# Four buffers instead of two for gathered rows, and an uneven split of the gathers between GpSimd and TensorE, in a four-layer graph network

## The chip, the core and the metric

The kernel runs on one core of a Trainium2 chip. The metric is device time in microseconds (us), the median of several executions. PE is TensorE, DVE VectorE, ACT ScalarE, POOL GpSimd and SP SyncE. The time before is 4519.79 us, the median of 3 runs (4518.19 to 4523.56).

## The reference, cut to what matters

There are 3125 nodes with 16 features and 100000 edges sorted by destination. Four layers follow each other, each on a layer-normed input and added to x:

```python
x = x + L0(h)   # edge network: message = h[src] times a 16x16 matrix made from the edge's attributes
x = x + L1(h)   # message = silu(tensor product of h[dst] and 8 edge attributes); summed by src
# L2: two relational convolutions
x_src = x[src]
msg   = sum over r of where(edge_type == r, x_src @ W[r], 0)
norm  = 1 / max(cnt[dst, edge_type], 1)
agg   = segment_sum(msg * norm, dst)
out   = agg + x @ root + bias
# L3
x   = features * out_deg ** -0.5
agg = zeros.at[dst].add(x[src]) * in_deg ** -0.5
```

So each phase gathers a row per edge by one index, weighs it, and sums it by another index.

## The kernel before, in words

The edges form 800 tiles of 125 edges, and 8 tiles form a chunk, so that there are 100 chunks and 50 pairs of chunks. The five phases are l0, l1, l2a, l2b (the two relational convolutions) and l3. Each walks over the 100 chunks. An even chunk uses slot s = 0 of the double-buffered tiles and an odd chunk uses slot s = 1.

The row of an edge reaches SBUF in one of two ways. A "far" tile is gathered by POOL with one indirect DMA of 125 rows (`gathers`, L610 to L626). A "near" tile is gathered on TensorE (`near_rows`, L785): a one-hot of the node's block of 25 nodes (made by DVE in `near_begin`, L1348, as bf16, L1354) times the node table split in three bf16 parts gives 25 candidate rows in PSUM, with 6 matmuls for a tile. DVE halves the candidates four times with predicated copies (`near_finish`, L1360, L1375) by the bits of the node's number. In l2a and l2b the near rows are then spread by edge type (L1409), turned by PE (`near_turn`, L800), copied by ACT (`near_copy`, L1023) and multiplied with the relation's weights by PE (`near_messages`, L807). For the far tiles of l2a and l2b the table in DRAM holds rows that are already multiplied. In l3 ACT copies the near rows into the tile of gathered rows (`near_place`, L1038). How many of a chunk's 8 tiles are near, for even and odd chunks, stands in `NEAR_OF` (L24); `far` (L291) is 8 less that.

For each chunk DVE weighs the rows into `msg` (L1585 near, L1588 far), splits them in three bf16 parts (`split`, L1264; its steps are called msg, hi, rest, mid, low) and spreads them into `stationary` (`to_stationary`, L1285, three instructions). Then PE adds the chunk to `acc` with 24 matmuls (`add_chunk`, L638). PE's order for chunk c in l2a and l2b is: additions of tiles 0 to 3, `near_turn(c+2)`, additions of tiles 4 and 5, `near_rows(c+3)`, additions of tiles 6 and 7, `near_messages(c+2)` (L839 to L852). DVE's order is: the chunk's own work, `is_lo` of c+1 (L1238), `near_finish(c+2)` with `near_begin(c+3)` between its steps (L1424).

Three waits set when POOL gathers for chunk c. The row numbers of c must have arrived (L615); SP loads them after all gathers of c-2 have landed (L431), in its own order after the fields of c-1, which wait for the step low of c-3 (L504), and the keys of c+1 (L499 to L509). And DVE must have read the slot's rows of c-2 (L618): that is the step msg in l2a and l2b, and the step low in l3 (`ROWS_READ`, L331). The loops over chunks have two unrolled chunks ahead, a body of two chunks, and the last four chunks unrolled (`near_chunks`, L359), for POOL none unrolled at the end (`all_chunks`, L341).

## Time and profile before

| | us |
|---|---|
| median of 3 runs | 4519.79 |
| the profiled execution | 4505.11 |
| its span, from the first to the last instruction | 4503.3 |
| PE busy | 4352.7 (97%) |
| DVE busy | 4112.4 (91%) |
| ACT busy | 3226.9 (72%) |
| POOL busy | 3272.0 (73%) |

The page lists the busy time of each engine, the busy share in 40 equal slices of the span, the chain of work that ended last, and the costliest groups of instructions with the idle time before them and what ended it. Five phases follow each other: l0 to about 1388 us, l1 to about 2279 us, l2a from 2337 to 3073 us, l2b from 3092 to 3825 us and l3 from 3841 to 4498 us. Only the last three are touched by the change.

### The profile page before, as it was taken

Reading aid. Unit: us, or ns where it says so; the run is one execution under the profiler, and the core shown is the slowest. Engines: PE = TensorE matmul, PEld = TensorE weight load, DVE = VectorE, ACT = ScalarE, POOL = GpSimd, SP = SyncE. Lnnn points to the kernel's source line nnn. Section 1 sums busy time; section 2 is a strip of 40 time slices with the busy share of each in tenths; the row PEclk is TensorE's granted clock in tenths of the full one; section 3 lists DMA queues with packets and bytes.
Section 4 is the critical chain, followed back from the end, with each engine's and each line's share of the span. In section 5 each row is a group of like instructions: output and inputs, shape, how many; then the busy total and the mean of one; then the engine's idle time right before and its main releaser. Section 6 shows DMA issues by size and latency. Waiting matters only on the chain.

```text
span 4503.3 us, 107817 instructions
## 1 busy us (share of the span) xinstructions
PE 4352.7 (97%) x30477; PEld 3243.1 (72%) x30477; DVE 4112.4 (91%) x11864; ACT 3226.9 (72%) x5359; POOL 3272.0 (73%) x2516
## 2 busy tenths in 40 slices
PE   6999999999997999999989999999999999799999
PEld 4777777777775777777757777776777777566666
DVE  7999999999997999999969999997999998788988
ACT  5777777777774777777737777776777777677777
POOL 6788888888884777777727776765777676688887
PEclk8999999999998999999989999999999999899999
DMA  2111111111112222222211111111111111111111
GB/s 59 28 17 18 18 17 18 17 18 17 18 17 50 62 61 61 61 61 61 61 36 27 27 27 26 28 27 40 28 27 28 27 27 22 32 30 31 31 30 26
DMA packets 337473, 148.67 MB, mean 33 GB/s; under 512 B 250582, under 2 KB 323074, under 8 KB 337434
## 3 DMA queue, kind: packets, MB, share of 16 engines
q0 software_dynamic: 104000, 59.31, 10.3%
q1 hardware_dynamic: 233434, 88.89, 8.0%
q8 instruction: 19, 0.31, 0.0%
q14 instruction: 20, 0.16, 0.0%
HBM read 135.45 MB, written 9.80 MB: 32 GB/s over the span
## 4 chain that ended last, share of the span: by engine, by line
PE 88%; DVE 5%; issue 3%; ACT 2%; DMA 1%; POOL 1%; SPq 0%; POOLq 0%; DVEq 0%; ACTq 0%
PE acc L638 42%; PE rows_ps L795 19%; PE rows_ps L725 7%; PE bank L811 5%; PE bank L725 4%; PE rows_ps L645 3%; PE eaT_ps L803 3%; DVE raw L1309 2%; PE rows_ps L713 2%; PE eaT_ps L701 1%; PE rows_ps L642 1%; ACT stack L970 1%; DVE ea_rest L1192 1%; ACT distances L911 0%; PE bank L671 0%
## 5 line engine op out<-in xcount | busy, mean ns | idle before, releaser
L638 PE MATMUL acc<-one_hot,stationary 125*128 125x392 bf16 x12000 | 2336.9, 329 | 38.5 <-issue 23.8
L622 POOL DMA_INDIRECT gathered<-table_l,row_numbers x1200 | 1601.8, 1335 | 433.6 <-issue 348.0
L638 PEld LDWEIGHTS acc<-one_hot,stationary 125*128 125x128 bf16 x12000 | 1156.0, 100 | 714.1 <-issue 45.7
L911 ACT ACTIVATE distances<-count_hi,fields 125x392 bf16<-125x392 f16 (+1 forms) x2500 | 1223.3, 558 | 0.0
L1285 DVE TENSOR_TENSOR stationary<-mask,parts 125x1024 bf16<-125x1024 bf16 x1500 | 944.1, 684 | 0.0
L896 ACT CAST mask<-is_lo 125x1024 bf16<-125x1024 f32 x500 | 522.2, 1044 | 528.1 <-issue 348.5
L622 POOL DMA_INDIRECT fields_all<-table_l,row_numbers x500 | 640.7, 1281 | 258.8 <-issue 123.2
L1257 DVE TENSOR_SCALAR one_hot<-count_hi,fields 125x392 bf16<-125x392 f16 x2300 | 740.8, 344 | 13.6 <-issue 13.5
L1375 DVE COPY_PREDICATED rows_ps<-near_bits_now,rows_ps 125x320 f32<-125x320 int8 (+3 forms) x1600 | 580.9, 363 | 161.9 <-PE rows_ps L795 119.7
L622 POOL DMA_INDIRECT gathered<-table_l2a,row_numbers x400 | 511.8, 1280 | 283.0 <-DVE parts L1267 117.5
L795 PE MATMUL rows_ps<-node_parts,h1T 125*125 125x192 bf16 (+1 forms) x7200 | 672.5, 251 | 21.5 <-DVE node_parts L1339 19.8
L795 PEld LDWEIGHTS rows_ps<-node_parts,h1T 125*125 125x125 bf16 x7200 | 655.4, 137 | 51.2 <-DVE node_parts L1339 20.0
L622 POOL DMA_INDIRECT gathered<-table_l2b,row_numbers x400 | 511.7, 1279 | 240.8 <-DVE parts L1267 115.3
L924 ACT ACTIVATE one_hot<-distances,ones 125x1568 bf16<-125x1568 bf16 (+1 forms) x400 | 674.0, 1685 | 6.6
L1028 ACT COPY h1T<-eaT_ps 128x500 f32<-128x500 f32 (+1 forms) x300 | 162.5, 542 | 345.3 <-PE eaT_ps L803 335.2
L1309 DVE TENSOR_REDUCE raw<-product 125x32 f32<-125x512 f32 x400 | 395.5, 1009 | 0.0
L725 PE MATMUL rows_ps<-w,h1T 128*125 128x256 f32 x1600 | 386.1, 385 | 7.6 <-DVE product L1302 5.8
L725 PE MATMUL bank<-w,h1T 128*125 128x256 f32 x1600 | 379.5, 380 | 0.0
L725 PEld LDWEIGHTS rows_ps<-w,h1T 128*125 128x125 f32 x1600 | 294.4, 189 | 57.4 <-DVE product L1302 7.4
L725 PEld LDWEIGHTS bank<-w,h1T 128*125 128x125 f32 x1600 | 301.8, 189 | 45.9
L1354 DVE TENSOR_SCALAR h1T<-near_key,node_key 125x500 bf16<-125x500 f16 (+1 forms) x800 | 317.8, 398 | 2.6 <-DMA near_key<-near_keys_by_chunk 2.5
L983 ACT ACTIVATE h1T<-rows_ps,b 128x500 f32<-128x500 f32 x400 | 249.3, 674 | 89.2 <-PE rows_ps L713 86.0
(216 smaller groups left out, 4704.6 us busy)
## 6 DMA issues: line engine op xcount, KB each, us to landing
near_key<-near_keys_by_chunk SPq DMA_DIRECT2D x300, 122.1 KB
gathered<-table_l,row_numbers POOLq DMA_INDIRECT x1200
fields<-edge_fields SPq DMA_DIRECT2D x500, 31.2 KB
near_key<-near_keys_by_chunk SPq DMA_DIRECT2D x100, 91.6 KB
fields_all<-table_l,row_numbers POOLq DMA_INDIRECT x500
gathered<-table_l2a,row_numbers POOLq DMA_INDIRECT x400
gathered<-table_l2b,row_numbers POOLq DMA_INDIRECT x400
ea<-in_edge_attr SPq DMA_DIRECT2D x100, 62.5 KB
```

The source lines that it names most:

```text
L622: pool.indirect_dma_start(out=gathered[ph][:, s, t, :], in_=table[ph], out_offset=None, in_offset=bass.IndirectOffsetOnAxis(ap=row_numbers ...
L638: mm = pe.matmul(acc[:, :], stationary[:, s, k, t, :, :].rearrange("p a b -> p (a b)"), one_hot[:, s, t, :], start=first and t == 0 and k ...
L725: mm = pe.matmul(bank[2 + q % 2][0:EP, j * HID:(j + 1) * HID], h1T[:, half, t * EP:(t + 1) * EP], w2[:, half, :], start=half == 0, stop=ha ...
L795: mm = pe.matmul(near_rows_ps[ph][s][:, t, 0:end - first, :].rearrange("p a f -> p (a f)"), near_one_hot[s][:, g, t * EP:(t + 1) * EP], pa ...
L896: act.copy(mask[:, s].rearrange("p t a f -> p (t a) f"), is_lo[:, s].rearrange("p t a -> p (t a)")[:, :, None].to_broadcast([EP, T * LO, F ...
L911: ins = act.activation(distances[:, i * n:(i + 1) * n], count_hi[:, 0:n], ACT.Abs, scale=-1.0, bias=fields[:, s, k, t:t + 1].bitcast(F32))
L924: act.activation(into, distances[:, 0:into.shape[1]], ACT.Relu, scale=-1.0, bias=ones[0:EP, 0:1]).then_inc(scalar_hot, 1)
L1257: dve.tensor_scalar(one_hot[:, s, t, :], count_hi[:, :], scalar_field(s, hi_field[ph], t), None, ALU.is_equal)
L1285: ins = dve.tensor_tensor(stationary[:, s, k], mask[:, s], source[:, s, :, k * F:(k + 1) * F][:, :, None, :].to_broadcast([EP, T, LO, F]), ...
L1309: dve.tensor_reduce(raw[:, s, 2 * q:2 * q + 2, :], product[:, q % 2].rearrange("p t i o -> p t o i"), AX.X, ALU.add).then_inc(products_sum ...
L1354: ins = dve.tensor_scalar(near_one_hot[s][:, g, 0:n], near_key[:, s, 0:n], node_key[:, g:g + 1], None, ALU.is_equal)
L1375: return dve.copy_predicated(into, chosen, source)
```

## The change

`gathered2`, the tile into which the rows of l2a, l2b and l3 are gathered, gets four slots instead of two, and chunk c uses slot c mod 4. POOL therefore waits for DVE's reading of chunk c-4 and not of c-2. There is one semaphore for each of the four slots, shared by the three phases. All other double-buffered tiles, the row numbers and fields among them, keep two slots. To know its slot of four at build time, every engine's loop over the chunks of these three phases now has a body of four chunks, with four chunks unrolled ahead and four behind (POOL: none behind). The odd chunks of l2a and l2b have three near tiles instead of four, so POOL gathers five tiles for them.

```diff
-NEAR_OF = {"l0": (0, 0), "l1": (3, 3), "l2a": (4, 4), "l2b": (4, 4), "l3": (4, 4)}
+QUADS = CHUNKS // 4
+NEAR_OF = {"l0": (0, 0), "l1": (3, 3), "l2a": (4, 3), "l2b": (4, 3), "l3": (4, 4)}
...
+class Slot(int):
+    def __new__(cls, four, quad):
+        self = int.__new__(cls, four % 2)
+        self.four, self.quad = four, quad
+        return self
+    def two_ago(self):
+        return Slot((self.four + 2) % 4, self.quad if self.four >= 2 else self.quad - 1)
...
-        rows2 = sb("gathered2", [ROWS, 2, T, F])
+        rows2 = sb("gathered2", [ROWS, 4, T, F])
...
+        def rows_in_by(ph, pair, s):
+            if ph not in FOUR_SLOTS:
+                return 16 * far(ph, s) * (pair + 1)
+            earlier = FOUR_SLOTS[:FOUR_SLOTS.index(ph)]
+            return 16 * QUADS * sum(far(k, s) for k in earlier) + 16 * far(ph, s) * (s.quad + 1)
...
+        def fours(eng, body, first, end, tail):
+            for chunk in range(4 * first):
+                body(chunk, chunk // 2, Slot(chunk % 4, chunk // 4))
+            with eng.Fori(first, end) as quad:
+                for j in range(4):
+                    body(4 * quad + j, 2 * quad + j // 2, Slot(j, quad))
+            for chunk in range(CHUNKS - tail, CHUNKS):
+                body(chunk, chunk // 2, Slot(chunk % 4, chunk // 4))
...
-        def near_chunks(eng, body):
+        def near_chunks(eng, body, ph="l1"):
+            if ph in FOUR_SLOTS:
+                fours(eng, body, 1, QUADS - 1, 4)
+                return
...
-                    sp.wait_ge(S[ph]["rows_in"][s], 16 * far(ph, s) * pair)
+                    if ph in FOUR_SLOTS:
+                        sp.wait_ge(S[ph]["rows_in"][s.two_ago().four], rows_in_by(ph, pair, s.two_ago()))
+                    else:
+                        sp.wait_ge(S[ph]["rows_in"][s], 16 * far(ph, s) * pair)
...
-                    if later(chunk, 2):
-                        pool.wait_ge(S[ph]["step"], done(ph, ROWS_READ[ph], chunk - 2))
+                    ahead = 4 if ph in FOUR_SLOTS else 2
+                    if later(chunk, ahead):
+                        pool.wait_ge(S[ph]["step"], done(ph, ROWS_READ[ph], chunk - ahead))
...
-                            out=gathered[ph][:, s, t, :], in_=table[ph], out_offset=None,
+                            out=gathered[ph][:, rows_slot(ph, s), t, :], in_=table[ph], out_offset=None,
...
-                all_chunks(pool, body)
+                if ph in FOUR_SLOTS:
+                    fours(pool, body, 1, QUADS, 0)
+                else:
+                    all_chunks(pool, body)
...
-                    dve.wait_ge(S[ph]["rows_in"][s], 16 * n * (pair + 1))
-                    st.mark(dve.tensor_tensor(msg[:, s, 0:n, :], gathered2[:, s, 0:n, :],
+                    dve.wait_ge(S[ph]["rows_in"][s.four], rows_in_by(ph, pair, s))
+                    st.mark(dve.tensor_tensor(msg[:, s, 0:n, :], gathered2[:, s.four, 0:n, :],
```

The calls of `near_chunks` on SP, PE, ACT and DVE pass the phase. The readers and writers of `gathered2` in l3 (`near_place`, the wait for the rows, `split`) take the slot of four in the same way.

## Rows read from the trace of the kernel before

**Rows 1.** The page, busy time of each engine over the span.
```profile
PE 4352.7 (97%) x30477; PEld 3243.1 (72%) x30477; DVE 4112.4 (91%) x11864; ACT 3226.9 (72%) x5359; POOL 3272.0 (73%) x2516
```

**Rows 2.** Stretches of l2a and l3: length, busy by engine, PE clock, DMA share, GB/s.
```profile
2400.00:3000.00 600.00, 600.00 (x4934) 469.00 (x4933) 556.40 (x1808) 433.54 (x658) 421.09 (x329) 1.00 0.17 27
...
3900.00:4450.00 550.00, 529.30 (x4119) 380.62 (x4118) 495.07 (x1546) 426.34 (x688) 440.85 (x344) 1.00 0.19 31
```

**Rows 3.** Chain of waits inside l2a: start us, us, what (parts of one chunk).
```profile
2408.81 2.00 PE acc L638 x12
2410.81 0.43 PE eaT_ps L803 x4
...
2412.23 2.06 PE rows_ps L795 x24
...
2415.29 0.78 PE bank L811 x8
```

**Rows 4.** POOL in l2a: start, us, operation, idle before and its releaser.
```profile
2705.30 1.48 POOL L622 DMA_INDIRECT gathered<-table_l2a,row_numbers  x1 [0.30 <-issue]
...
2711.11 1.21 POOL L622 DMA_INDIRECT gathered<-table_l2a,row_numbers  x1 [1.29 <-DVE parts L1267]
```

**Rows 5.** POOL in the first chunks of l2a, and DVE's first wait for rows.
```profile
2337.62 1.21 POOL L622 DMA_INDIRECT gathered<-table_l2a,row_numbers  x1 [72.45 <-DMA table_l2a<-stage]
...
2343.77 1.21 POOL L622 DMA_INDIRECT gathered<-table_l2a,row_numbers  x1 [0.30 <-issue]
2344.93 0.23 DVE L1588 TENSOR_TENSOR msg<-gathered,edge_norm 125x64 f32<-125x64 f32 x1 [2.18 <-DMA gathered<-table_l2a,row_numbers]
...
2354.39 1.36 POOL L622 DMA_INDIRECT gathered<-table_l2a,row_numbers  x1 [0.30 <-issue]
...
2373.03 1.21 POOL L622 DMA_INDIRECT gathered<-table_l2a,row_numbers  x1 [0.30 <-DMA row_numbers<-edge_fields]
```

**Rows 6.** Groups by line in l3, 3900 to 4450: count, busy, mean ns, idle before.
```profile
L622 POOL DMA_INDIRECT gathered<-table_l,row_numbers x344 | 442.2, 1285 | 109.4 <-issue 102.7 <-DVE is_lo L1238 6.4 <-DMA row_numbers<-in_src 0.3
```

**Rows 7.** Timeline of l3: a gather that begins with the spreading of parts.
```profile
4223.76 1.89 DVE L1285 TENSOR_TENSOR stationary<-mask,parts 125x1024 bf16<-125x1024 bf16 x3
...
4223.79 1.73 POOL L622 DMA_INDIRECT gathered<-table_l,row_numbers  x1 [0.30 <-issue]
```

**Rows 8.** Groups by line in l0, 600 to 1265, same columns as rows 6.
```profile
L622 POOL DMA_INDIRECT gathered<-table_l,row_numbers x400 | 543.7, 1359 | 122.0 <-issue 106.8 <-DVE rest L1270 15.2
```

**Rows 9.** Timeline at the ends of l2a and of l3.
```profile
3058.76 1.21 POOL L622 DMA_INDIRECT gathered<-table_l2a,row_numbers  x1 [0.30 <-issue]
...
3072.95 0.57 DVE L1597 COPY aggT<-acc 128x392 f32<-128x392 f32 x1 [5.17 <-PE acc L638]
...
4487.30 1.48 POOL L622 DMA_INDIRECT gathered<-table_l,row_numbers  x1 [0.31 <-issue]
...
4497.77 0.57 DVE L1636 COPY aggT<-acc 128x392 f32<-128x392 f32 x1 [4.25 <-PE acc L638]
```

**Rows 10.** Waits in l3, 3900 to 4450: total us, times, longest us.
```profile
DVE rows_ps L1375 <- PE rows_ps L795: 24.5, 43, 0.6
DVE one_hot L1257 <- issue: 12.6, 43, 0.3
```

**Rows 11.** Timeline of l3: POOL's first wait, and DVE reading gathered rows.
```profile
3857.76 1.39 POOL L622 DMA_INDIRECT gathered<-table_l,row_numbers  x1 [4.12 <-DVE parts L1276]
...
4210.15 0.51 DVE L1267 CAST parts<-gathered 125x128 bf16<-125x128 f32 x1
```

**Rows 12.** Timeline of l2a: DVE's last split step, and SP's loads for later chunks.
```profile
2704.21 0.29 DVE L1276 TENSOR_TENSOR parts<-rest,parts 125x128 bf16<-125x128 f32 x1
...
2706.59 0.01 SPq L436 DMA_DIRECT2D row_numbers<-edge_fields  x1
```

**Rows 13.** Timeline of l2a: DVE's spreading by type, and its wait for near rows.
```profile
2706.85 0.49 DVE L1375 COPY_PREDICATED rows_ps<-near_bits_now,rows_ps 125x320 f32<-125x320 int8 x1 [0.41 <-PE rows_ps L795]
...
2709.00 0.69 DVE L1409 TENSOR_TENSOR fields_all<-rows_ps,near_is_type 125x512 f32<-125x512 f32 x1
```

More of the change, by code:

```diff
@@ L240, in build, with rows_slot @@
         S = {}
+        FOUR_SLOTS = ("l2a", "l2b", "l3")
+        rows_in_four = [sem(f"rows_in{q}") for q in range(4)]
         for ph in PHASES:
             S[ph] = {
-                "rows_in": [sem(f"{ph}_rows_in{s}") for s in range(2)],
+                "rows_in": rows_in_four if ph in FOUR_SLOTS else [sem(f"{ph}_rows_in{s}") for s in range(2)],
                 "step": sem(f"{ph}_vector_step"),
             }
+        def rows_slot(ph, s):
+            return s.four if ph in FOUR_SLOTS else s
+        def rows_in_by(ph, pair, s):
[3 more added lines that the diff above has]
+            return 16 * QUADS * sum(far(k, s) for k in earlier) + 16 * far(ph, s) * (s.quad + 1)
         fields_in = [sem(f"fields_in{s}") for s in range(2)]
@@ L509, in body @@
                         load_near_keys(ph, chunk + 2, s)
-                near_chunks(sp, body)
+                near_chunks(sp, body, ph)
             def stream_l0():
@@ L622, in body @@
                         pool.indirect_dma_start(
-                            out=gathered[ph][:, s, t, :], in_=table[ph], out_offset=None,
+                            out=gathered[ph][:, rows_slot(ph, s), t, :], in_=table[ph], out_offset=None,
                             in_offset=bass.IndirectOffsetOnAxis(ap=row_numbers[:, s, t:t + 1], axis=0),
-                        ).then_inc(S[ph]["rows_in"][s], 16)
-                all_chunks(pool, body)
+                        ).then_inc(S[ph]["rows_in"][rows_slot(ph, s)], 16)
+                if ph in FOUR_SLOTS:
+                    fours(pool, body, 1, QUADS, 0)
+                else:
+                    all_chunks(pool, body)
             for ph in PHASES:
@@ L852, in body @@
                         near_messages(ph, chunk + 2, s)
-                near_chunks(pe, body)
+                near_chunks(pe, body, ph)
             sum_near("l1")
@@ L1036, in near_bits_of, with near_place @@
                 act.copy(near_bits_now[:, s, 0:NEAR_OF[ph][s]].bitcast(I8), bits.bitcast(I8)).then_inc(near_bits_in, 1)
-            def near_place(chunk, s):
+            def near_place(chunk, four):
+                s = four % 2
                 act.wait_ge(near_picked, chunks_before("l3") + chunk + 1)
-                act.copy(gathered2[:, s, far("l3", s):T, :], near_rows_ps["l3"][s][:, 0:NEAR_OF["l3"][s], 0, :]).then_inc(ev("l3_near_placed"), 1)
+                act.copy(gathered2[:, four, far("l3", s):T, :], near_rows_ps["l3"][s][:, 0:NEAR_OF["l3"][s], 0, :]).then_inc(ev("l3_near_placed"), 1)
             def masks_and_near(ph):
@@ L1059, in body @@
                     if later(chunk, 1) and follows(chunk, 1):
-                        near_result(chunk + 1, 1 - s)
+                        near_result(chunk + 1, (s.four + 1) % 4 if ph == "l3" else 1 - s)
                     if ph == "l1":
@@ L1068, in body @@
                         near_bits_of(ph, chunk + 3, 1 - s)
-                near_chunks(act, body)
+                near_chunks(act, body, ph)
             def preload(column, function):
@@ L1429, in body @@
                         near_finish(ph, chunk + 2, pair + 1, s, follows(chunk, 3))
-                near_chunks(dve, body)
+                near_chunks(dve, body, ph)
             dve.wait_ge(added, before("l0") + CHUNKS)
@@ L1628, in l3 @@
                 hot(0, 1)
-                dve.wait_ge(S["l3"]["rows_in"][s], 16 * far("l3", s) * (pair + 1))
+                dve.wait_ge(S["l3"]["rows_in"][s.four], rows_in_by("l3", pair, s))
                 dve.wait_ge(ev("l3_near_placed"), chunk + 1)
-                split(st, gathered2[:, s], lambda k: hot(*((2, 3), (4, 5), (6, 7), ())[k]))
+                split(st, gathered2[:, s.four], lambda k: hot(*((2, 3), (4, 5), (6, 7), ())[k]))
                 to_stationary("l3", chunk, s, parts, lambda: st.wait("low"))
```

## The prediction, written before the changed kernel ran

> **What bounds the kernel now.** I read the page first. PE is busy 97% of the span and DVE 91%, POOL only 73% [rows 1]. That is an average over five phases, so I went to the stretches. Inside l2a PE is busy for 600.00 of 600 us, DVE for 556.40 and POOL for 421.09. In l3 PE is at 529.30 of 550 and POOL at 440.85 [rows 2]. The clock is at its upper level (2.4 GHz) in both.
>
> Then the chain of waits inside l2a. It never leaves PE, and one chunk in it is 24 additions, the turning of 4 tiles (0.43), the near rows of 4 tiles (2.06) and their messages (0.78) [rows 3]. The stretch holds 329 gathers, four to a chunk, so a chunk takes 600 / (329/4) = 7.30 us and a pair 14.60. L2a and l2b are bound by PE; l2b is l2a over again.
>
> A busy share hides POOL's state, so its timeline came next. In l2a a gather is busy 1.21 us and 0.30 us of idle follows it always, even with nothing to wait for. Over seven undisturbed steps that is (2354.39 - 2343.77) / 7 = 1.517 us for a gather [rows 5]. Each chunk also has one gather of 1.48, and an idle of 1.29 that ends with DVE's reading of c-2 [rows 4]. Less the usual 0.30, that leaves POOL only 0.99 us free per chunk of 7.30. In l3 POOL has none: its 344 gathers in 550 us are 1.599 us each, made up of 1.285 busy and 0.318 idle [rows 6]. "80% busy" is a full POOL here.
>
> **The odd chunks' fourth near tile.** It leaves PE: a quarter of the turning, of the near rows and of the messages, (0.43 + 2.06 + 0.78) / 4 = 0.82 us per pair [rows 3]. PE would need 14.60 - 0.82 = 13.78 us per pair. DVE is relieved as well (fewer candidate columns in its four halvings, and L1409 a quarter narrower [rows 13]). I estimate 0.4 us per pair, against a message multiplication that is one tile wider; I cost it at nothing because PE and POOL lie above it.
>
> POOL gets one more gather per pair, nine instead of eight. Undisturbed this is 9 x 1.517 = 13.65 us. The gathers are disturbed, though. One that begins 0.03 us after DVE's spreading of parts (L1285) takes 1.73 instead of 1.21 us [rows 7], and the one in the middle of it takes 1.48 [rows 4]. So each chunk costs POOL between 0 and 0.52 us more. In the first 24 gathers of l2a, which wait for nothing, it is nearly nothing: (2373.03 - 2337.62) / 23 = 1.540 us each [rows 5]. In l3, where POOL is full as it would be now, a gather's mean is 1.285, so 0.073 over the undisturbed 1.212 (the busy part of the 1.517) [rows 6]. In l0, where DVE has more work of this kind, the mean is 1.359, so 0.147 over [rows 8]. I take l3's value, whose DVE work per chunk is nearest: 9 x (1.517 + 0.073) = 14.31 us per pair. This is above PE's 13.78, so **POOL becomes the bound of l2a and l2b**, at 14.31 instead of 14.60.
>
> **From pairs to the phase.** POOL starts a phase at the same place as before, when the table is stored. Before, it took 3059.97 - 2337.62 = 722.35 us for the phase's gathers, since it ran ahead in the first six chunks [rows 5, 9]. Now it takes 50 x 14.31 = 715.5: 6.85 less. What lies behind the last gather shrinks too. In l2a it was 3072.95 - 3059.97 = 12.98 us, because DVE and PE were behind POOL. In l3, where DVE waits for the last rows, it was 4497.77 - 4488.78 = 8.99 [rows 9], and l2's longer way from rows to parts adds about 0.3. So 3.7 us go. That makes 10.5 us per phase and 21 us for both.
>
> **Four buffers.** POOL's wait for c-2 goes. What is late next is the row numbers. SP issued them 2.09 us after the step low of c-3 had ended (2706.59 against 2704.50 [rows 12]); with 1.5 us for landing, an estimate from a gather that ended at 2343.47 and whose rows DVE could read at 2344.93 [rows 5], they are there at 3.6. The gather used to begin 6.6 us after that step (2711.11 [rows 4]). POOL may thus be some 3 us earlier, and no more, since the numbers keep two slots. With POOL as the bound this wait is never late, and neither would the old one have been: rows of c-2 are read within 2 us of their landing while POOL is busy 6 us and more with c-1. In l2 the buffers cost and bring about nothing by themselves. Queued behind POOL's waits are only further gathers.
>
> In l3 the wait of 4.12 us at 3857.76 goes [rows 11]. At that point PE's first additions, not the rows, were late. In steady state the waits hide in POOL's idle of 0.318 instead of 0.305, about 0.05 us per chunk. The chunk there is 6.40 us, and DVE does not wait for gathered rows: its idle is for near rows (24.5 us) and 43 times 0.3 us of "issue" in front of the one-hots, which is once per pair of chunks and so looks like the loop's jump [rows 10]. A body of four chunks halves these jumps, 25 x 0.29 = 7 us if all of them count. DVE is not alone on that path, so I take 3. The bounds for l3 are -20 us (a chunk falls to PE's 529.30 / 86 = 6.15, with some left over) and +10 (another meeting of gathers and DVE work; DVE's reading at 4210.15 is already stretched to 0.51 [rows 11]).
>
> **The sum.** 21 + 3 = 24 us. The profiled execution took 4505.1 us, so it becomes 4481. The median of the runs lies 14.7 above that execution; I let this stand and predict 4519.8 - 24, about **4495 us**.
>
> **A rule against this change.** A gather is stretched while DVE runs L1285 [rows 7]. The Trainium skill, page "SBUF — State Buffer", section "Who interferes with whom", says that whoever takes the port pair shared by DVE and GpSimd first holds it for the whole instruction and the other is fully blocked. By this, the stretch ends with one of the three instructions, which agrees with 0.52, less than one instruction's 0.68. The same section infers that a tensor_tensor should not block descriptor generation; by that no gather of these phases would be stretched by L1285, and the sum would be the best case of the second rival. The trace speaks against it with its 1.73.
>
> **The rivals.**
> 1. *The same change with POOL hardly disturbed.* The first chunks of l2a speak for it: 9 x 1.540 = 13.86 us per pair, 693 us for a phase, so 29.4 + 3.7 = 33 less. Both phases and l3 give 69 less: 4451. Undisturbed altogether, PE's 13.78 holds: 41 per phase, 4435. Against it: those chunks were at the start, and l2's steady state and l3 both show stretched gathers. 13%.
> 2. *l3 gains too*, because POOL's phase against DVE comes free and PE becomes its bound: 20 more, 4475. For it: PE is 96% busy there. Against: POOL at 1.517 + 0.073 needs 6.36 of 6.40 us anyhow. 10%.
> 3. *It moves nothing.* DVE, PE and POOL all stand within 0.8 us of each other per pair, DVE waits 0.41 for near rows, and PE's turning needs DVE's L1409 [rows 13]; small waits of one for another eat the gain. At 14.49 us per pair (0.42 of stretch per chunk) a phase keeps only 1.6 us: 4514. 19%.
> 4. *POOL becomes a worse bound than PE was.* The place is the gather loop of l2a and l2b, and the mechanism is that every gather meets DVE's work as in l0: 1.517 + 0.147 = 1.664 us, 14.98 per pair, 749 us per phase, 26.4 - 3.7 = 23 more. Both give 46 more: 4563 with l3's 3 off. It decides from 14.52 us per pair, or 1.613 per gather, where the phase is as long as before. For it: POOL's margin is 0.3 per pair only. Against it: l0's DVE has eight one-hots and a wide key mask per chunk, l2's four. 11%.
>
> The forecast has the remaining 47%, and its own range is 4482 to 4510.
>
> **How the numbers follow.** A difference under 0.2% (9 us) can't be told from none. Faster: the forecast but for its upper end (0.43), rivals 1 and 2 (0.23), and a part of 3 (0.04): 0.70. Within: the rest of the forecast and most of 3, 0.19. Slower: 0.11. The range reaches from 4468 to 4521; left out are rival 4 and most of rival 1.
>
> **What would show it.** Right: in l2a and l2b POOL has no idle over 0.45 us between the first gather and the last, about 1.59 us from gather to gather, PE shows idle time of 2 to 4%, and DVE waits for gathered rows at L1588. The odd chunks' near rows have 18 matmuls. From the first gather to the reading of acc the phases take some 725 and 723 us. Wrong: POOL still waits in each chunk (then the numbers' way over SP, or the DVE-PE handshake, is the bound), or the mean gather is over 1.31 us busy, which makes it slower. In l3, L1257's "issue" idle should come half as often; if the phase's length moves by more than 8 us, my reading that POOL's slot wait doesn't bind it is wrong.

## The result and the profile after

The changed kernel took 4553.91 us (median of 7 runs, 4545.32 to 4560.23); the kernel before, timed beside it, 4523.33 (7 runs, 4518.19 to 4534.62). The ratio is 1.0064, 95% interval 1.0053 to 1.0076: slower by 0.6%, where 4495 and a range up to 4521 had been forecast. The profiled execution took 4553.76 us, so this profile stands for its median.

Later in the study the same changed kernel took 4497.70 us on another chip, beside a kernel before of 4504.27 (ratio 0.9991, 0.9977 to 1.0004). Most of what follows is about these two numbers. A series is a set of kernels timed on one chip, with the kernel before among them. I call the chips on which the kernel before takes 4523 to 4525 us **kind A** (three series, the result's among them), and those on which it takes 4502 to 4504 **kind B** (three series, on three chips). No chip is known to stand in two series, so it is not shown whether the kind belongs to the chip or to the time at which it was used; read "kind of chip" with that in mind.

Busy time on the page of the changed kernel, kind A (answers to [rows 1]):

```profile
PE 4296.7 (94%) x29577; PEld 3158.3 (69%) x29577; DVE 4142.9 (91%) x11864; ACT 3203.9 (70%) x5359; POOL 3408.3 (75%) x2616
```

PE was relieved as planned: from 4352.7 to 4296.7 us, 56 less (0.56 us for each of the 100 odd chunks; 0.82 had been forecast), and POOL has its 100 gathers more. But PE is idle 6% of the time, and no other engine has filled up. The stretches of l2a and of l3 (answer to [rows 2], same columns):

```profile
2400.00:3000.00 600.00, 563.51 (x4458) 424.61 (x4456) 554.28 (x1765) 417.52 (x643) 463.83 (x364) 1.00 0.17 25
3950.00:4500.00 550.00, 526.65 (x4092) 378.17 (x4091) 497.60 (x1536) 424.14 (x685) 446.28 (x341) 1.00 0.19 31
```

364 gathers at nine to a pair are 600 / (364/9) = 14.84 us per pair, against 14.60 before and 14.31 forecast. The groups of gathers by line over the whole phases:

```profile
L664 POOL DMA_INDIRECT gathered<-table_l2b,row_numbers x450 | 575.9, 1280 | 201.2 <-issue 120.6 <-DMA row_numbers<-edge_fields 33.6 <-DMA table_l2b<-stage 28.7
L664 POOL DMA_INDIRECT gathered<-table_l2a,row_numbers x450 | 575.6, 1279 | 236.4 <-issue 119.0 <-DMA table_l2a<-stage 72.9 <-DMA row_numbers<-edge_fields 33.8
```

A gather's mean is 1.279 us, so nine with the usual 0.303 of idle are 9 x 1.582 = 14.24 us, even a little under the 14.31 of the forecast. POOL could have done it. It waits instead. Over the whole of l2a 22 of its idles are longer than 0.45 us (33.1 us together), in l2b 33 (45.5 us), and 17 and 20 of them end with the arrival of row numbers. The waits in l2a, 2400 to 3000 (us in total, times, longest):

```profile
POOL gathered L664 <- DMA row_numbers<-edge_fields: 30.7, 34, 2.6
...
ACT h1T L1073 <- remote: 41.7, 12, 4.2
...
DVE rows_ps L1421 <- remote: 17.9, 22, 2.2
DVE rows_ps L1421 <- PE rows_ps L840: 11.5, 20, 0.7
...
PE eaT_ps L848 <- DVE fields_all L1455: 16.8, 21, 1.5
```

DVE and ACT wait for PE, while PE itself waits at the turning. The timeline shows how that goes together (start us, us, what, idle before):

```profile
2563.22 0.65 PE L848 MATMUL eaT_ps<-ident,fields_all 125*128 125x125 f32 x4 [0.74 <-issue]
...
2564.70 1.71 PE L840 MATMUL rows_ps<-node_parts,h1T 125*125 125x208 bf16 x18
...
2566.53 0.58 ACT L1073 COPY h1T<-eaT_ps 128x500 f32<-128x500 f32 x1 [3.45 <-remote]
...
2569.83 0.41 DVE L1421 COPY_PREDICATED rows_ps<-near_bits_now,rows_ps 125x240 f32<-125x240 int8 x1 [2.16 <-remote]
...
2572.31 0.54 PE L848 MATMUL eaT_ps<-ident,fields_all 125*128 125x125 f32 x3 [1.41 <-issue]
```

By the record PE ended the turning at 2563.87, but ACT, idle until then, copied it only at 2566.53; the near rows ended at 2566.41 and DVE, idle from 2567.67, took them at 2569.83. The trace also holds the semaphore updates. DVE's arrive 0.01 us after the end of their instruction. PE's, between 2450 and 3000, arrive 0.71 us after the recorded end for the additions, 0.89 for the near rows, 0.50 for the turning and 0.70 for the messages on average, up to 4.7. In the trace of before only the near rows' were late, by 0.46 on average and 0.57 at most; the others came after 0.014. The ends of matmuls are modelled in a trace, so this can't say whether the results were finished later or reported later. Their starts do not show a slower PE: additions in a row start 0.166 us after one another (median) in both traces. The granted clock is 1.00 in both. At first I took these delays for the work of the change alone. The later traces say otherwise: in the changed kernel on kind B they are 0.25, 0.58, 0.03 and 0.03 us in the same stretch, and in the kernel before on kind A 0.014, 0.58, 0.014 and 0.014. So the long delays need both, the kind and the change.

### The profile page after: what moved, and what is told of

Its sections match the earlier page's. It is cut to its first block, busy times and chain, and to the rows that moved or that the text cites. A ratio compares the mean times of both kernels' runs of the same rounds, so it can differ in the third digit from the quotient of the medians.

```text
span 4552.0 us, 104968 instructions
## 1 busy us (share of the span) xinstructions
PE 4296.7 (94%) x29577; PEld 3158.3 (69%) x29577; DVE 4142.9 (91%) x11864; ACT 3203.9 (70%) x5359; POOL 3408.3 (75%) x2616
## 4 chain that ended last, share of the span: by engine, by line
PE 66%; DVE 17%; issue 10%; ACT 3%; another core or an unknown queue 2%; DMA 1%; DVEq 1%; POOL 1%; SPq 0%; ACTq 0%; POOLq 0%
PE acc L683 29%; PE rows_ps L840 13%; PE rows_ps L770 8%; PE bank L770 4%; DVE stationary L1331 3%; PE rows_ps L690 3%; DVE one_hot L1303 3%; PE bank L856 2%; PE rows_ps L758 2%; DVE raw L1355 2%; DVE rows_ps L1421 2%; PE eaT_ps L848 2%; PE eaT_ps L746 1%; PE rows_ps L687 1%
## 5 line engine op out<-in xcount | busy, mean ns | idle before, releaser
L1303 DVE TENSOR_SCALAR one_hot<-count_hi,fields 125x392 bf16<-125x392 f16 x2300 | 799.3, 369 | 6.1 <-issue 6.0
L664 POOL DMA_INDIRECT gathered<-table_l2a,row_numbers x450 | 575.6, 1279 | 236.4 <-issue 119.0
L664 POOL DMA_INDIRECT gathered<-table_l2b,row_numbers x450 | 575.9, 1280 | 201.2 <-issue 120.6
L1421 DVE COPY_PREDICATED rows_ps<-near_bits_now,rows_ps 125x128 f32<-125x128 int8 (+5 forms) x1600 | 561.8, 351 | 169.3 <-PE rows_ps L840 70.0
L840 PE MATMUL rows_ps<-node_parts,h1T 125*125 125x208 bf16 (+1 forms) x6600 | 621.1, 251 | 23.3 <-DVE node_parts L1385 21.6
L840 PEld LDWEIGHTS rows_ps<-node_parts,h1T 125*125 125x125 bf16 x6600 | 603.7, 137 | 53.8 <-DVE node_parts L1385 22.6
L1073 ACT COPY h1T<-eaT_ps 128x375 f32<-128x375 f32 (+1 forms) x300 | 151.6, 505 | 431.3 <-PE eaT_ps L848 305.6
L1400 DVE TENSOR_SCALAR h1T<-near_key,node_key 125x375 bf16<-125x375 f16 (+1 forms) x800 | 297.2, 373 | 2.4 <-DMA near_key<-near_keys_by_chunk 2.3
```

What stands on the lines that cost most here:

```text
L664: pool.indirect_dma_start(out=gathered[ph][:, rows_slot(ph, s), t, :], in_=table[ph], out_offset=None, in_offset=bass.IndirectOffsetOnAxis ...
L840: mm = pe.matmul(near_rows_ps[ph][s][:, t, 0:end - first, :].rearrange("p a f -> p (a f)"), near_one_hot[s][:, g, t * EP:(t + 1) * EP], pa ...
L1303: dve.tensor_scalar(one_hot[:, s, t, :], count_hi[:, :], scalar_field(s, hi_field[ph], t), None, ALU.is_equal)
L1400: ins = dve.tensor_scalar(near_one_hot[s][:, g, 0:n], near_key[:, s, 0:n], node_key[:, g:g + 1], None, ALU.is_equal)
L1421: return dve.copy_predicated(into, chosen, source)
```

## The experiments

Times are medians; each ratio is to the kernel before on the same chip.

**1. Which part of the change costs.** Four kernels on a chip of kind A (before 4523.35).

Only the near tiles: the kernel before with

```
NEAR_OF = {..., "l2a": (4, 3), "l2b": (4, 3), ...}
```

> Two slots and bodies of two chunks as before; only the odd chunks of l2a and l2b have three near tiles. What the changed kernel's trace shows: PE's semaphore updates come late, up to 4.7 us after the matmul's end in l2a and l2b (mean 0.7, before 0.15). Theory A, the body of four chunks on PE makes them late: here they come in time, the gain that I predicted appears, about 20 us faster than before. Theory B, a PE with less work and gaps between its matmuls makes them late: about 25 to 30 us slower, as the whole change. Theory C, POOL kept busy without a pause does it, whatever the buffers: slower too, since nine gathers per pair fill POOL here as well; if only four slots keep it busy enough, the same as before within 10 us.

Measured: 4589.34, ratio 1.0153 (1.0130 to 1.0177): the direction of theory B, and twice its 25 to 30 us.

Only the buffers and the bodies of four chunks: the changed kernel with

```
NEAR_OF = {..., "l2a": (4, 4), "l2b": (4, 4), ...}
```

> Four slots and bodies of four chunks, but four near tiles in every chunk of l2a and l2b, as before. Theory A (body of four on PE): late updates in l2a and l2b, 10 to 30 us slower. Theory B (gaps in PE): none in l2, since PE has its full work; l2 as before within 5 us in all. Theory C (POOL without a pause): POOL still pauses in l2, so l2 is as before; l3 is 4 us longer as in the changed kernel.

Measured: 4535.19, ratio 1.0030 (1.0018 to 1.0042). Theory B's "l2 as before within 5 us" did not hold: l2a and l2b took 764.6 and 769.1 us from start to start, where the kernel before on kind A takes 755.9 and 752.6 (series 3 below); l3 was shorter, 665.1 against 679.3.

The changed kernel with two buffers of gathered rows (bodies of four stay):

```
-        rows2 = sb("gathered2", [ROWS, 4, T, F])
+        rows2 = sb("gathered2", [ROWS, 2, T, F])
...
-                    ahead = 4 if ph in FOUR_SLOTS else 2
+                    ahead = 2
...
```

> As the changed kernel (bodies of four, three near tiles in odd chunks) but the rows go to two slots and POOL waits for chunk c-2, as before. If the slots matter (theory C in its narrow form): about 20 us faster than before. If the body of four or the uneven split does it (A or B): about 30 us slower, as the changed kernel.

Measured: 4546.73, ratio 1.0055 (1.0034 to 1.0076).

The changed kernel with PE's loop in pairs:

```
-                near_chunks(pe, body, ph)
+                near_chunks(pe, body)
```

> The changed kernel, but PE alone walks the relational phases and l3 in bodies of two chunks, as before. Theory A (the body of four on PE): updates in time, about 20 us faster than before. Theories B and C: about 30 us slower, as the changed kernel.

Measured: 4557.76, ratio 1.0078 (1.0055 to 1.0100).

What follows: on this chip the near tiles alone are a loss of 66 us, and PE's long body is not its cause, since the kernel with the old body is the slowest. The edit of the near tiles relieves PE and gives POOL a ninth gather per pair; which of the two costs was never separated on kind A. Four buffers against two make no difference that these runs show, with bodies of four (4553.9, 4545 to 4560, on its own chip, against 4546.7, 4546 to 4567). The bodies of four help here: with two buffers and three near tiles in both, they take 43 us off (4589.3 to 4546.7). Why is open.

**2. PE's relief and POOL's load apart.** Four kernels on a chip of kind B (before 4502.62). At the time I did not know that this mattered.

Three near tiles on PE, but no fifth gather:

```
+        def fetched(ph, s):
+            return min(far(ph, s), 4) if ph in FOUR_SLOTS else far(ph, s)
...
-                    for t in range(far(ph, s)):
+                    for t in range(fetched(ph, s)):
```

The counts of landed gathers follow `fetched` too, and the tile that is never fetched is set to zero once; the kernel leaves that tile's messages out.

> The changed kernel without the fifth gather of the odd chunks (l2a, l2b): PE still takes only three near tiles there, POOL gathers four tiles per chunk, and the message of tile 4 multiplies a row that is never fetched (that tile's messages are left out of the result). Theory P, the ninth gather per pair fills POOL and every late row number is lost time: POOL needs 8 x 1.58 = 12.7 us per pair, PE 13.9, so a pair goes from 14.84 (after) to about 14.0: l2a and l2b 40 us shorter each than after, 4475 us, faster than before. Theory Q, PE's shorter work opens gaps in it and the chain between PE, DVE and ACT runs badly with them, whatever POOL does: 4545 to 4560 as in the changed kernel.

Measured: 4454.06, ratio 0.9883 (0.9863 to 0.9903).

Four near tiles, with a fifth gather in odd chunks that nothing reads:

```
+            return 5 if ph in ("l2a", "l2b") and s == 1 else far(ph, s)
...
-                            out=gathered[ph][:, rows_slot(ph, s), t, :], ...
+                            out=gathered[ph][:, rows_slot(ph, s), t, :] if t < far(ph, s) else unused[0:EP, s.four, :], ...
```

> Four buffers, PE takes four near tiles in all chunks of l2a and l2b (as before), but POOL issues a fifth gather in the odd chunks into a tile that nothing reads. Theory P: POOL's ninth gather per pair is the cost, so l2a and l2b are as long as in the changed kernel (739 and 748 us from first to last gather) or longer, since PE needs 14.6: 4550 to 4580. Theory Q: PE has its old load and few gaps, POOL has 14.24 us of work in a pair of 14.7: within 8 us of the kernel with four buffers alone, 4535 to 4543.

Measured: 4537.19, ratio 1.0083 (1.0061 to 1.0104). In microseconds this lies in theory Q's range; but all these expectations were counted from a kernel before of 4523, and as a ratio to before it is in P's range (4550 to 4580 over 4523, 1.006 to 1.013) and above Q's.

Row numbers in four buffers, loaded two chunks earlier:

```
+                sp.wait_ge(S[ph]["rows_in"][ago.four], rows_in_by(ph, pair, ago))
+                load_into_four(ph, chunk + 2, ago.four)
```

> The changed kernel, with row numbers in four buffers too (l2a, l2b, l3): SP loads those of chunk c+2 where it loaded those of c, so POOL may run four chunks ahead. Theory P: POOL's idle over 0.45 us (33 and 45 us in l2a and l2b) goes, POOL runs at 14.24 us per pair, and l2a and l2b come to about 712 us between first and last gather: 27 and 36 less, 4490 to 4500. Theory Q: POOL's waits are a consequence; it waits elsewhere or finishes early, and the time stays at 4545 to 4560.

Measured: 4489.36, ratio 0.9974 (0.9964 to 0.9984). POOL has no idle over 0.45 us, and from first to last gather l2a and l2b take 713.7 and 711.9 us; this profile is of the fastest of the nine runs, 4476.06.

The same with four near tiles everywhere:

> Four near tiles in all chunks, four buffers for rows and for row numbers. Theory P: with eight gathers per pair POOL has time to spare, the numbers come in time either way, and it is within 10 us of the kernel with four buffers of rows alone (4535). A third theory R, a gather that runs earlier meets DVE and PE at other places and this decides: it moves by over 10 us in one direction or the other, and POOL's mean gather changes from 1.300 us.

Measured: 4511.02, ratio 1.0018 (1.0009 to 1.0028).

I read this as proof that the late row numbers made the loss (4554 to 4489). That reading compared two chips.

**3. Early numbers with two buffers of rows, and one trace more of before** (kind A, before 4525.25). The edit of the first is that of the third kernel of 1, made on the kernel with early numbers.

> The kernel with row numbers in four buffers, but gathered rows in two (so POOL waits for the reading of chunk c-2 again), three near tiles in odd chunks. Theory P1, only the row numbers' way over SP made POOL late: as with four buffers of rows (4489 against a before of 4503, ratio 0.997), POOL without idle over 0.45 us, 712 us from first to last gather. Theory P2, the wait for the reading of c-2 is late too once the numbers are early, because a burst of five gathers needs its start on time: POOL's idle comes back at DVE's step msg, l2a and l2b at 725 us or more, ratio 1.000 to 1.006. My prediction's sentence (rows of c-2 are read within 2 us of landing while POOL is busy 6 us with c-1) is P1.

Measured: 4563.91, ratio 1.0077 (1.0056 to 1.0099). By this P2 would hold; in 5, on a chip of kind B, it fell. On kind A four buffers with early numbers were never run beside it, so there it stays open.

> The kernel before, unchanged, with a second profile, as a measure of how far one kernel's profiled executions differ. If they are alike: l2a and l2b start to start 754.5 and 749.2 us as in the first, PE's semaphore updates on time (0.01 us, near rows 0.4), l3 from its first gather to the end 662 us. If the kernel before has several steady states: phases longer by 5 to 20 us and late updates as in the kernels with three near tiles.

Measured: 4524.13, one run. l2a and l2b took 755.9 and 752.6 us from start to start, as in the first trace, but l3 679.3 where that had 662.0. With this trace the chips first showed. L1 is the same code in every kernel here and equally long (917 to 921 us). ACT's wait for PE's turning there, 1500 to 2200, in the first trace of before and in this one:

```profile
ACT h1T L1028 <- PE eaT_ps L803: 113.9, 79, 1.6
```

```profile
ACT h1T L1028 <- PE eaT_ps L803: 180.5, 82, 2.3
```

1.44 us a time in the first, 2.20 in the second. Over all twenty traces of this study the sum is 112 to 118 us in thirteen and 173 to 182 in seven, with nothing between: the seven are those from the series of kind A. The first trace of before is one of the thirteen; its execution, 4505.11 us, also lies outside the 4518 to 4535 of the timed runs beside it. **The profile from which I predicted was of the other kind of chip than the runs by which I was measured.**

**4. Two combinations that were missing, a shorter tie, and the changed kernel again** (kind B, before 4504.27).

Early numbers, three near tiles, no fifth gather (the edit of the first kernel of 2):

> Row numbers in four buffers, three near tiles in odd chunks on PE, but POOL without the fifth gather there (tile 4 of odd chunks multiplies a row that is never fetched; its messages are left out of the result). Theory P, PE and DVE could do a pair in about 13.9 us if POOL never bound them and always had what it waits for: l2a and l2b 700 to 705 us from start to start less the 28 us of the ends, 4445 to 4460, at or slightly under the kernel without the fifth gather and with numbers in two buffers (4454). Theory V, early rows are bad for PE and DVE by themselves: slower than that kernel, over 4465.

Measured: 4444.67, ratio 0.9872 (0.9854 to 0.9891), as theory P had it.

Early numbers, four near tiles, a fifth gather that nothing reads (the edit of the second kernel of 2):

> Row numbers in four buffers, four near tiles in all chunks, and a fifth gather in the odd chunks into a tile that nothing reads. With PE at 14.60 us per pair and POOL at 14.28. Theory P: POOL has 0.3 us to spare per pair and is never late, so it is as without the ninth gather: 4511 (4505 to 4520). Theory W, nine gathers per pair cost DVE and PE through stretched instructions wherever they fall: 10 us or more above 4511.

Measured: 4532.23, ratio 1.0070 (1.0054 to 1.0087): theory W, 21 us above the same kernel without the ninth gather, 4511.

Early numbers, POOL waits for c-3 (`ahead = 3`):

> The kernel with row numbers in four buffers (three near tiles, nine gathers per pair), but POOL waits for the reading of chunk c-3 in place of c-4. In the trace with four, a gather began 4.6 to 6.2 us after the reading of c-2 in every chunk, so neither wait ever held it there. Theory P: one chunk less makes no difference, 0.997 of before. Theory S, the fast pace is one of two states and a tie to DVE's reading, even one that is rarely reached, lets it fall into the slow one: as with two buffers, 1.004 or more of before.

Measured: 4488.80, ratio 0.9967 (0.9954 to 0.9980): P, one buffer less does nothing.

The changed kernel, unedited:

> The changed kernel once more, on the chip of the other three, since its time (4553.9, 1.0064 of before) was taken on another chip than those with numbers in four buffers. If chips do not matter: 1.0064 of before within 0.002, l2a and l2b 765 to 780 us from start to start. If they do: 1.000 to 1.003, and the gain of the early numbers is smaller than it looks.

Measured: 4497.70, ratio 0.9991 (0.9977 to 1.0004). This is neither of the two I had written down: the chip decides over 56 us.

**5. Four kernels side by side** (kind B again, before 4502.46), the same as above: early numbers; early numbers with two buffers; buffers and bodies of four only; near tiles only.

> The kernel with row numbers in four buffers (three near tiles in odd chunks), beside the next three on one chip. Theory C, there are two kinds of chips, and on those where the kernel before takes 4523 PE's results reach the others late in any kernel with idle time on PE: on such a chip 4530 to 4550 (1.002 to 1.006 of before), on one where the kernel before takes 4503 as measured there, 4489. Theory P, the tie by the row numbers made the loss of the changed kernel: 4485 to 4510 on either.

> Early row numbers with two buffers of rows, on one chip with four. Theory C: what separated them (4564 against 4489) was mostly the chip; here they lie within 25 us of each other. Theory P2, the wait for the reading of c-2: 50 us or more apart, on either kind of chip.

> Four buffers of rows and bodies of four chunks, four near tiles everywhere. Where the kernel before takes 4523: 4535 as measured. Where it takes 4503: theory C gives 4505 to 4515 (as with early numbers, 4511), since POOL's waits cost nothing beside PE's 14.60 us per pair; a cost of the buffers of its own would make it 4520 or more.

> The kernel before with three near tiles in the odd chunks of l2a and l2b, nothing else. Where the kernel before takes 4523: 4589 as measured. Where it takes 4503: theory C gives 4500 to 4530, since the changed kernel is at 4498 there; if two buffers and a burst of five gathers are bad by themselves, 4550 or more.

Measured: 4492.86 (0.9979, 0.9968 to 0.9991), 4488.54 (0.9972, 0.9960 to 0.9984), 4508.49 (1.0010, 1.0001 to 1.0020) and 4490.25 (0.9974, 0.9965 to 0.9984). Theory C has the first three; the first lies in theory P's range as well, and the last came out 10 us below C's 4500 to 4530. What theory C says of early numbers on kind A (4530 to 4550) was never run. P2 falls on this kind, and the reading of 2 falls: within kind B the early numbers are worth 5 to 9 us (4498 to 4493 and 4489), not 64. The medians in one table:

```
                                        kind A      kind B
before                                 4523-4525   4502-4504
near tiles only                           4589        4490
buffers and bodies of four only           4535        4508
both (the change)                         4554        4498
both, two buffers of rows                 4547          -
both, early numbers                         -       4489, 4493
both, early numbers, two buffers          4564        4489
near tiles relieved, no ninth gather        -         4454
```

The kernel with the near tiles alone is the clearest case, the same instructions on both kinds of chip, 99 us apart. L2a, 2400 to 3000, on kind A and on kind B (length, busy times of PE, PEld, DVE, ACT, POOL, clock, DMA):

```profile
2400.00:3000.00 600.00, 559.01 (x4376) 418.19 (x4377) 540.04 (x1737) 410.47 (x631) 449.90 (x355) 0.99 0.16 25
```

```profile
2400.00:3000.00 600.00, 580.35 (x4628) 439.58 (x4627) 580.55 (x1832) 430.24 (x665) 481.76 (x378) 1.00 0.18 26
```

A gather is busy 449.90/355 = 1.267 us on the one and 1.274 on the other, and DVE's spreading 0.685 on both. The mean granted clock of the two executions is 0.984 and 0.984; the 0.99 against 1.00 in this stretch is too little for the 6% between them (355 and 378 gathers). What differs is DVE's waits for the near rows in that stretch, kind A and then kind B:

```profile
DVE rows_ps L1375 <- remote: 28.0, 21, 2.9
DVE rows_ps L1375 <- PE rows_ps L795: 16.2, 32, 1.0
```

```profile
DVE rows_ps L1375 <- PE rows_ps L795: 3.3, 7, 0.6
DVE rows_ps L1375 <- remote: 2.8, 6, 0.5
```

44.2 us against 6.1. And POOL, tied to DVE by its two buffers, waits in turn, again A and then B:

```profile
POOL gathered L622 <- DVE parts L1267: 55.9, 45, 3.6
```

```profile
POOL gathered L622 <- DVE parts L1267: 13.7, 34, 1.3
```

PE's semaphore updates there come 1.25 us (A) and 0.35 us (B) after the recorded ends of the near rows, and 0.87 and 0.01 us after those of the messages.

## Why the prediction was wrong, step by step

**The step that failed** is the term "10.5 us per phase and 21 us for both", and in it the sentence "With POOL as the bound this wait is never late". On kind A, where the comparison was made, both phases became longer instead. From the first gather of one phase to that of the next (l3: to the end of the program), in the two traces of kind A:

| us | before (series 3) | changed | forecast |
|---|---|---|---|
| l2a | 755.9 | 767.8 (+11.9) | -10.5 |
| l2b | 752.6 | 778.3 (+25.7) | -10.5 |
| l3 | 679.3 | 667.9 (-11.4) | -3 |

Together that is 26.2 of the 29.7 us between the two spans (4522.3 and 4552.0). The gathers themselves kept to the forecast: 450 x (1.279 + 0.305) = 713 us in each, where 715.5 was taken. But the first to the last gather took 739.1 and 748.4 us, and POOL's idles over 0.45 us make up the difference (33.1 and 45.5 us, less 0.305 each for the usual idle, are 26.4 and 35.4). Mostly row numbers ended them. SP, which loads these, was held up by the other engines: in 600 us of l2a it waited 145.6 us for ACT's `distances` and 1.3 us for the gathers of c-2, where on kind B it waited 87.9 and 22.0.

Under that step lies another sentence: "The median of the runs lies 14.7 above that execution; I let this stand". I took 14.7 us for an offset that both kernels share. The traces put it down to two kinds of chip (before: 20 us apart), and the change meets them very differently: +30.6 us on one, -6.6 on the other. Every duration in my sum came from kind B; the comparison was made on kind A. The kernel before hides this in l2, where its PE is full: it is 1.4 and 3.4 us longer there on kind A, and 17.3 us longer in l3. Its l2a on kind A:

```profile
2400.00:3000.00 600.00, 600.00 (x4923) 466.23 (x4922) 551.71 (x1804) 432.45 (x657) 419.98 (x329) 1.00 0.17 27
```

**Held against the right kind,** the steps come out like this. The gathers in the changed kernel on kind B, and their stretch of l2a:

```profile
L664 POOL DMA_INDIRECT gathered<-table_l2b,row_numbers x450 | 575.3, 1278 | 169.2 <-issue 118.3 <-DMA table_l2b<-stage 29.4 <-DVE parts L1313 9.7
L664 POOL DMA_INDIRECT gathered<-table_l2a,row_numbers x450 | 573.8, 1275 | 215.7 <-issue 119.8 <-DMA table_l2a<-stage 71.9 <-DMA row_numbers<-edge_fields 11.3
```

```profile
2400.00:3000.00 600.00, 578.89 (x4605) 437.57 (x4605) 574.02 (x1827) 430.64 (x664) 479.32 (x377) 1.00 0.18 26
```

- *POOL's rate.* Right: 1.275 and 1.278 us of a gather where 1.285 was taken from [rows 6]. From the first gather to the last, l2a took 717.6 us and l2b 715.1; the forecast was 715.5. POOL has 7 and 3 idles over 0.45 us, where I expected none. PE is idle 3.5% of the stretch, within the 2 to 4% forecast. One sign did not come: between 2400 and 3000 DVE never waits for gathered rows. So POOL runs at its full rate, but that DVE and PE only follow it is not shown; the rows lie ready for some 5 us when DVE reads them.
- *The phases.* From start to start l2a went from 754.5 to 747.0 and l2b from 749.2 to 742.0 us: 7.5 and 7.2 less, where 10.5 each had been forecast. The tail behind l2a's last gather shrank by 2.7 us (32.1 to 29.4 up to the next phase's first), not by 3.7. From first to last gather l2b had been 2.0 us shorter before than the l2a that I used for both.
- *PE.* 0.56 us per pair by its own records on kind A, 0.60 on kind B (4293.1 us busy), instead of 0.82. By the forecast's own rule PE, with 14.0 us per pair, still lies under POOL's 14.31.
- *The wait for row numbers.* "With POOL as the bound this wait is never late" is nearly true on kind B:

```profile
POOL gathered L664 <- DMA row_numbers<-edge_fields: 9.7, 25, 1.4
```

  On kind A it is 30.7 us in 34 times. The old wait for c-2, of which the prediction says that it would not have been late either, is the one of the kernel with the near tiles alone: 5 and 1 idles over 0.45 us in l2a and l2b on kind B, but 37 and 35 (58.0 and 53.4 us) on kind A.
- *"Rows of c-2 are read within 2 us of their landing"* was wrong on either kind. DVE's reading begins 6.7 us after the end of a chunk's last gather on average on kind B and 7.7 on kind A, some 5 and 6 us after the landing with the prediction's 1.5 us for that; in the trace of before it was 7.44 us. Only in the first run of the kernel with early numbers was it 1.5 to 2.3 us. It explains nothing of the result by itself: two buffers and early numbers run as fast as four on kind B.
- *l3.* Forecast 3 us less; measured on kind B 6.7 more (662.0 to 668.7 from its first gather to the end of the program), and the gather's mean rose from 1.287 to 1.319. The halved loop jumps did come: the waits of L1303 for "issue" are 19 in 500 us, against 43 in 550 before. They gave nothing. The bound of +10 was there for this: another meeting of gathers and DVE's work. The longer gathers fit that, but no run isolates it. On kind A l3 was shorter after the change, 679.3 to 667.9, as in every kernel there with bodies of four (665 to 668).
- *The sum, on kind B:* 7.5 + 7.2 - 6.7 = 8.0 us less in the three phases, 7.6 between the two spans (4503.3 and 4495.7), 6.6 by the medians; 24 had been forecast. Of the 16 us missing, 9.7 are l3 and 6.3 the two phases. So even on kind B the forecast had the direction and a third of the size.

**The rivals.** Rival 3 (small waits of DVE, PE and POOL for one another eat the gain) describes kind A best, but I let it end at "nothing moves". Rival 4 forecast 4563, near the measured 4554, by another mechanism: a gather of 1.359 us, where 1.279 was measured. Its number is no credit. Rival 2 wanted 20 us more from l3; on kind B l3 lost 6.7, on kind A it gained 11.4 while the rest lost. Rival 1 fell: a gather and its idle took 1.58 us on either kind, not 1.540. In the paragraph on the rule against the change, "second rival" should read first: POOL undisturbed is the best case of rival 1.

**What the parts are worth.** These differences are of medians from three chips of kind B (before 4502.5 to 4504.3), some of four runs that spread by up to 22 us, so a few us mean nothing. On kind B the parts add up: the near tiles give 12 us and the buffers with their bodies of four cost 6, together the 6.6 measured. Within the near tiles, PE's relief alone is worth 4508 - 4454 = 54 us, and the ninth gather takes 4498 - 4454 = 44 of it back. With PE at four near tiles the ninth gather costs 4537 - 4508 = 29 us though POOL has room for it (14.24 in 14.60 us), so not all of its price is POOL as the bound. With early numbers the three are 66, 44 and 21. DVE's one-hots stretch with the ninth gather (from 0.369 to 0.381 us each, four per chunk), which is some 10 of the 29 us at most. On kind A the parts do not add up: +66 and +12 make +31.

**What stays open.** Why PE's results arrive late on kind A, and most so in the kernels with three near tiles: there the updates of the additions in l2a come 0.70 to 0.81 us late on average in all five, in the two with four near tiles 0.014 and 0.20, and on kind B 0.014 to 0.30 in all thirteen. That PE's gaps are the reason is a guess; PE's relief without a ninth gather was never run on kind A. Nor does a PE that is not full suffice: in l3 the kernels with bodies of four take as long on kind A (665 to 668 us) as on kind B (659 to 669). The trace can't tell a slower PE from a later report. In l1 each update of the turning comes 0.8 to 0.9 us later, and l1 is as long as on kind B, which a PE that computed slower all the time would not allow. The granted clock shows no difference; the Trainium skill, page "TensorE: Matmul & The Clock Gate", section "Seeing it yourself", warns that the clock's trace events on trn2 have been seen to be unreliable, and no run here decides whether they are. That POOL's tie to DVE and to the row numbers amplifies the loss on kind A is argued from the order of waits, not shown: early numbers with four buffers were never run there.

**A better version.** On kind B the kernel with near tiles alone (4490, 0.9974) and the changed one with early row numbers (0.9967 to 0.9979 in three series, three or four buffers of rows) beat both. The first loses 66 us on kind A, the second has no time there, and its sister with two buffers of rows loses 39. Nothing here is shown to be faster than the kernel before on both kinds.

## What to carry to other kernels

Check that the profile you predict from belongs to the runs you are compared with: a profiled execution outside the spread of the timed runs is a warning, and a wait in a phase that the change does not touch (here ACT's for PE's turning in l1) is a fingerprint by which traces can be sorted. Compare experiments only on one chip, or repeat one kernel in every series; I drew a wrong conclusion from two series before I did. Where engines are nearly equally full and hand work back and forth, a sum of their busy times does not give the time: taking 0.6 us per pair from the fullest engine was worth 54 us alone, 12 with the gather that pays for it, and -66, with that gather, on a chip where one engine's results come late.

## What the runs showed of the hardware

- Two kinds of chips: the same kernels take 20 us (before), 27 (buffers only), 56 (the change), 75 (early numbers, two buffers) and 99 us (near tiles only) more on one than on the other, though DVE's spreading takes 0.685 us on either and additions on PE start 0.166 us after one another, with a mean granted clock of 0.984 in both executions of the last. Within a series the kernel before kept to its kind: its runs lie between 4510 and 4535 us on kind A and between 4493 and 4513 on kind B.
- PE's semaphore updates can come up to 4.7 us after the end that the trace gives its matmul, while DVE's come after 0.01. In these traces a wait of DVE or ACT for "remote", while PE's record has long ended, is such a late update.
- An indirect gather of 125 rows costs POOL 1.51 us undisturbed (1.21 busy, 0.30 idle), the same on both kinds; its mean was 1.261 to 1.323 busy in all kernels of this study in l2 and l3. DVE's one-hots (L1303) took 0.400 us on average in l2a of the changed kernel, up to 0.736, against 0.317 in the trace of before. The number of gathers is not all of it: with eight per pair, buffers and bodies of four make it 0.369, and early numbers bring it back to 0.322.
